# Two-layer convolution-attention kernel: which engine forms the neighbour sums of the second half of the batch, and in which order the second layer follows

## The reference, cut to what matters

```python
x = x + dilated_attention(group_norm(x))     # first layer
x = x + channel_attention(group_norm(x))     # second layer
```

```python
attn = softmax_over_9(q * shifted(k) summed over a head's channels * scale)
out  = sum_over_9(attn[n] * shifted(v, n)) * gate[s]
```

## Time and profile before

| what | value |
|---|---|
| device time, median of 3 runs | 83.1 us (83.1 to 83.11) |
| the profiled execution's own time | 83.13 us |
| span of that execution in the trace | 81.3 us |
| around the span (start and end) | 1.8 us |
| PE busy | 71.1 us (87%) |
| DVE busy | 67.5 us (83%) |
| POOL busy | 41.5 us (51%) |
| ACT busy | 29.3 us (36%) |
| share of the chain that ended last | DVE 54%, PE 28%, POOL 7% |

### The profile page before, as it was taken

The page is one execution under the profiler, slowest core; times in us unless marked ns, Lnnn a source line. Parts: engine busy times, 40 slices in busy tenths (PEclk is TensorE's granted clock), DMA queues, the critical chain, the costliest instruction groups (busy, mean ns, idle before and its releaser), DMA issues.

```text
span 81.3 us, 2474 instructions
## 1 busy us (share of the span) xinstructions
PE 71.1 (87%) x1010; PEld 51.4 (63%) x1010; DVE 67.5 (83%) x184; ACT 29.3 (36%) x92; POOL 41.5 (51%) x84
## 2 busy tenths in 40 slices
PE   4999998799995698999969797879999999999950
PEld 4999753466742466776857664567676868575530
DVE  2152999999999989999999699889999888597850
ACT  1762765963384000000030003230994271764200
POOL 7104018912930037999999999699990005100000
PEclk9999999999999999999999999999999999999999
DMA  1980055000000000000000000000000000012253
GB/s 27 315 286 18 0 120 142 7 0 8 0 0 4 0 12 0 0 0 4 8 0 0 0 0 0 8 0 0 0 0 8 0 0 12 0 57 72 73 194 129
DMA packets 2796, 3.06 MB, mean 38 GB/s; under 512 B 352, under 2 KB 2400, under 8 KB 2784
## 3 DMA queue, kind: packets, MB, share of 16 engines
q1 hardware_dynamic: 2496, 2.63, 10.5%
q10 hardware_dynamic: 288, 0.26, 0.9%
HBM read 1.84 MB, written 1.05 MB: 36 GB/s over the span
## 4 chain that ended last, share of the span: by engine, by line
DVE 54%; PE 28%; POOL 7%; issue 5%; ACT 2%; POOLq 0%
PE ps L815 27%; DVE qk L602 18%; DVE pv L643 12%; POOL rstd L342 3%; POOL acc L379 3%; DVE acc L655 3%; DVE pv L655 2%; DVE x L674 2%; DVE prob L622 2%; DVE smax L609 2%; DVE ssum L619 2%; POOL pv L379 2%; DVE sums L570 1%; DVE acc L643 1%; PE ps L972 1%
## 5 line engine op out<-in xcount | busy, mean ns | idle before, releaser
L815 PE MATMUL ps<-prob,sel 64*128 64x192 f32 (+6 forms) x192 | 17.8, 313 | 2.7 <-DVE pv L643 1.6
L643 DVE TENSOR_TENSOR pv<-ps,v 128x128 f32<-128x128 f32 (+7 forms) x32 | 17.1, 567 | 1.8 <-PE ps L815 0.8
L815 PEld LDWEIGHTS ps<-prob,sel 64*128 64x128 f32 x192 | 13.7, 186 | 6.9 <-DVE pv L643 3.5
L815 PE MATMUL ps<-xn,wp 128*32 128x256 f32 (+1 forms) x208 | 17.1, 384 | 0.9 <-ACT q L417 0.7
L815 PE MATMUL ps<-idle 128*128 128x128 f32 x82 | 14.6, 328 | 1.1 <-DVE idle L533 1.1
L379 POOL TENSOR_TENSOR pv<-pv 128x240 f32<-128x240 f32 (+3 forms) x24 | 14.1, 600 | 0.5 <-DVE pv L643 0.5
L815 PEld LDWEIGHTS ps<-idle 128*128 128x128 f32 x82 | 12.6, 231 | 2.4 <-DVE idle L533 1.1
L342 POOL TENSOR_TENSOR rstd<-gvar,mhalf 128x2 f32<-128x2 f32 (+1 forms) x6 | 4.9, 809 | 15.9 <-DVE gvar L549 15.9
L379 POOL TENSOR_TENSOR acc<-acc,pv 128x256 f32<-128x256 f32 (+4 forms) x20 | 12.7, 640 | 0.5
L815 PEld LDWEIGHTS ps<-xn,wp 128*32 128x32 f32 (+1 forms) x208 | 8.7, 116 | 6.1 <-ACT xn L443 1.3
L602 DVE TENSOR_TENSOR qk<-q,k 128x672 f32<-128x672 f32 (+7 forms) x21 | 11.4, 607 | 0.0
(11 more groups left out here) (82 smaller groups left out, 89.6 us busy)
## 6 DMA issues: line engine op xcount, KB each, us to landing
out_dram<-x SPq DMA_DIRECT2D x8, 128.0 KB, 1.8
gx<-x_dram SPq DMA_DIRECT2D x2, 256.0 KB, 4.4
gx<-x_dram ACTq DMA_DIRECT2D x2, 128.0 KB, 3.1
sel<-selc_dram SPq DMA_DIRECT2D x4, 64.0 KB, 2.2
wp<-wpack_dram SPq DMA_DIRECT2D x1, 194.0 KB, 4.2
gx<-x_dram SPq DMA_DIRECT2D x1, 192.0 KB, 2.8
wp<-wpack_dram SPq DMA_DIRECT2D x1, 131.0 KB, 2.2
gx<-x_dram SPq DMA_DIRECT2D x1, 128.0 KB, 3.0
```

What stands on the lines that cost most here:

```text
L643: last = nc.vector.tensor_tensor(o, a, b, ALU.mult)
L815: return nc.tensor.matmul(o, w, m, start=start, stop=stop)
```

## The change

PE takes over the sums of (1,2) and (1,3) almost wholly, and the second half of (0,3). POOL keeps all 8 additions of (0,0), (0,1), (0,2), (1,0), (1,1) and the first 4 of (0,3). DVE's 8 additions of (1,2) and 2 of (1,3) become 6 small ones behind its last product (`add_last`). `restore` and `sum_second` are replaced by `add_tiles`, which takes products in 32x32 tiles for phase 0 (all four slots j at once) and for phase 1 (two slots j at a time: first batches 1 and 3, then 5 and 7). PE's second-layer work of groups 0 and 1, but for two projections, moves behind these sums, and so does DVE's and ACT's; five calls of `keep_clock` on a group's bank go; one `norm` moves from ACT to DVE; the inverse roots of groups 0 and 1 stand behind other additions of POOL.

The bodies of the functions that go stand in the code above, and the indentation is shortened.

```diff
@@ -31,15 +31,15 @@
 X_PIECES = ((0,), (2,), (4,), (6,), (1, 3), (5, 7))
 ARRIVAL = (0, 2, 6, 4, 1, 3, 5, 7)
 X_ORDER = (0, 2, 4, 6, 1, 3, 5, 7)
-NORMS_ON_DVE = ((2, 0), (3, 0), (3, 1))
-NORMS_ON_ACT = ((0, 0), (0, 1), (1, 0), (1, 1), (2, 1))
+NORMS_ON_DVE = ((2, 0), (2, 1), (3, 0), (3, 1))
+NORMS_ON_ACT = ((0, 0), (0, 1), (1, 0), (1, 1))
 PT_ON_DVE = ((2, 0), (2, 1))
 PT_ON_ACT = ((0, 0), (0, 1), (1, 0), (1, 1), (3, 0), (3, 1))
 MT_ON_DVE = ((0, 0), (3, 1))
 MT_ON_ACT = ((0, 1), (1, 0), (1, 1), (2, 0), (2, 1), (3, 0))
-POOL_SUMS = (ND, 2)
-RSQRT_AFTER = ((1, 0, 4), (1, 1, 0))
+POOL_ADDS = ((8, 8, 8, 4), (8, 8, 0, 0))
+RSQRT_AFTER = ((1, 1, 1), (1, 1, 3))
 F32 = mybir.dt.float32
@@ -86,8 +86,12 @@
     return [(t, a, f) for (t, a), f in zip(pairs, after)]
-ADDS = len(additions(0))
 ADD_NEEDS = (1, 2, 2, 2, 3, 3, 3, 3)
+def added_by(ph, s):
+    return sum(POOL_ADDS[0]) * ph + sum(POOL_ADDS[ph][:s + 1])
 def valid_rows(s, ri):
@@ -217,7 +221,6 @@
 spread_ready = sem("spread_ready")
 pv_ready = sem("pv_ready")
 added = sem("added")
-dve_added = sem("dve_added")
 last_added = sem("last_added")
 restored = sem("restored")
 xn1_act_ready = sem("xn1_act_ready")
@@ -366,10 +369,10 @@
     link(nc.gpsimd.tensor_tensor(gsel[:], gpick[:, :, 0], gpick[:, :, 1], ALU.add))
     nc.gpsimd.tensor_tensor(gate[:], gsel[:], grec[:], ALU.mult).then_inc(gate_ready, 1)
-    base = 0
     for ph in range(PHASES):
-        for s in range(POOL_SUMS[ph]):
-            for n, (target, slot, after) in enumerate(additions(s)):
+        for s in range(ND):
+            base = added_by(ph, s) - POOL_ADDS[ph][s]
+            for n, (target, slot, after) in enumerate(additions(s)[:POOL_ADDS[ph][s]]):
                 chunk = 12 * ph + 3 * s + ADD_NEEDS[n]
                 if n == 0 or ADD_NEEDS[n] > ADD_NEEDS[n - 1]:
                     pool.wait_ge(pv_ready, chunk)
@@ -380,7 +383,6 @@
                 if (ph, s, n) in RSQRT_AFTER:
                     g = RSQRT_AFTER.index((ph, s, n))
                     rsqrt(PHASES + g, group(g))
-            base += ADDS
     for g in range(len(RSQRT_AFTER), GROUPS):
         rsqrt(PHASES + g, group(g))
@@ -492,29 +494,29 @@
     for i in range(2):
         norm(0, i)
     for i in range(2):
+        copy_projection(0, i)
+    for i in range(2):
         norm(1, i)
-    for i in range(2):
-        copy_projection(0, i)
-    copy_projection(1, 0)
-    for i in range(2):
-        copy_pT(0, i)
-    copy_projection(1, 1)
-    for i in range(2):
-        copy_pT(1, i)
-    attention_exp(0)
-    attention_exp(1)
     squares(2)
     squares(3)
+    for i in range(2):
+        copy_pT(0, i)
+    for i in range(2):
+        copy_projection(1, i)
+    copy_projection(2, 0)
+    attention_exp(0)
+    copy_projection(2, 1)
+    for i in range(2):
+        copy_pT(1, i)
+    for i in range(2):
+        copy_projection(3, i)
+    attention_exp(1)
     copy_fused(0, 1)
-    copy_fused(1, 0)
-    norm(2, 1)
-    copy_fused(1, 1)
-    for g in range(2, 4):
-        for i in range(2):
-            copy_projection(g, i)
-    copy_pT(3, 0)
+    for i in range(2):
+        copy_pT(3, i)
     attention_exp(2)
-    copy_pT(3, 1)
+    for i in range(2):
+        copy_fused(1, i)
     attention_exp(3)
     for i in range(2):
         copy_fused(2, i)
@@ -631,7 +633,9 @@
             dve.wait_ge(proj_copied, tiles.index((2, s, ph)) + 1)
         dve.wait_ge(spread_ready, c + 1)
         if ph and chunk == 0:
-            dve.wait_ge(added, ADDS * (s + 1))
+            dve.wait_ge(added, added_by(0, s))
+            if s == LAST_UNIT:
+                dve.wait_ge(restored, SLOTS)
         c0, c1, co = columns(DIL[s], ci)
         nc_ = c1 - c0
         for n, ri, dri, r0, dr, a0, da, rows in pieces(s):
@@ -643,27 +647,17 @@
             last = nc.vector.tensor_tensor(o, a, b, ALU.mult)
         last.then_inc(pv_ready, 1)
-    def add_neighbours(ph, s):
...
-    def add_last_column():
...
+    def add_last():
+        steps = ((2, 7, 6, 0), (3, 7, 6, 0), (2, 1, 0, 0), (2, 7, 8, 1), (3, 7, 8, 2), (2, 1, 2, 3))
         dve.wait_ge(pv_ready, 12 * PHASES)
-        for n, ri in enumerate((0, 2)):
+        for s, onto, slot, after in steps:
+            ci, ri = divmod(slot, 3)
             r0, r1 = valid_rows(s, ri)
-            c0, c1, _ = columns(DIL[s], 2)
-            o, a = (pv[s][:, slot, :].rearrange("p (r c) -> p r c", c=W)[:, r0:r1, c0:c1] for slot in (middle, 6 + ri))
-            if n:
-                dve.wait_ge(last_added, n)
+            c0, c1, _ = columns(DIL[s], ci)
+            o, a = (pv[s][:, n, :].rearrange("p (r c) -> p r c", c=W)[:, r0:r1, c0:c1] for n in (onto, slot))
+            if after:
+                dve.wait_ge(last_added, after)
             nc.vector.tensor_tensor(o, o, a, ALU.add).then_inc(last_added, 1)
     def first_residual(g):
@@ -764,40 +758,40 @@
         multiply_pv(1, 0, i)
     multiply_pv(1, 1, 0)
     first_residual(0)
-    multiply_pv(1, 1, 1)
+    first_residual(1)
+    for i in range(1, 3):
+        multiply_pv(1, 1, i)
     second_variance(0)
-    first_residual(1)
-    multiply_pv(1, 1, 2)
+    multiply_pv(1, 2, 0)
     second_variance(1)
-    for i in range(2):
-        multiply_pv(1, 2, i)
+    multiply_pv(1, 2, 1)
     second_norm_bias(0)
-    second_norm_bias(1)
     multiply_pv(1, 2, 2)
     multiply_pv(1, 3, 0)
-    add_neighbours(1, 2)
+    second_norm_bias(1)
     for i in range(1, 3):
         multiply_pv(1, 3, i)
-    add_last_column()
+    add_last()
+    first_residual(2)
+    second_variance(2)
+    first_residual(3)
+    second_norm_bias(2)
+    for i in range(2):
+        norm(2, i)
+    second_variance(3)
     attention_shift(0)
+    second_norm_bias(3)
+    for i in range(2):
+        norm(3, i)
+    attention_divide(0)
+    for i in range(2):
+        copy_pT(2, i)
+    copy_fused(0, 0)
     attention_shift(1)
-    attention_divide(0)
-    first_residual(2)
-    first_residual(3)
-    copy_fused(0, 0)
-    second_variance(2)
     attention_divide(1)
-    second_variance(3)
-    second_norm_bias(2)
-    norm(2, 0)
-    second_norm_bias(3)
-    for i in range(2):
-        norm(3, i)
-    copy_pT(2, 0)
-    second_residual(0, 0)
-    copy_pT(2, 1)
-    second_residual(0, 1)
     attention_shift(2)
+    for i in range(2):
+        second_residual(0, i)
     attention_divide(2)
     attention_shift(3)
     second_residual(1, 0)
@@ -913,43 +907,23 @@
             last = mm(o, sel[half:half + 64, j % 2, s, :], m)
         last.then_inc(spread_ready, 1)
-    def restore(g):
...
-    def sum_second():
...
+    def add_tiles(ph, tiles, js, stop, finished=False):
+        for s, slot in tiles:
+            if slot == 4:
+                t, first, (r0, r1), (c0, c1) = acc, (ph * ND + s) * N, (0, H), (0, W)
+            else:
+                ci, ri = divmod(slot, 3)
+                t, first, (r0, r1), (c0, c1) = pv[s], slot * N, valid_rows(s, ri), columns(DIL[s], ci)[:2]
             dims = [[W, r1 - r0], [1, c1 - c0]]
             at = r0 * W + c0
-            for j in range(SLOTS):
+            for j in js:
                 rows = slice(32 * j, 32 * j + 32)
-                last = mm(view(ps, 512 * (BANK[2] + j) + at, dims, 32 * s, 32), ident[rows, rows],
-                          view(t, first + at, dims, 32 * j, 32), start=start, stop=stop)
-                if stop and s == LAST_UNIT:
+                last = mm(view(ps, 512 * (BANK[GROUPS // PHASES * ph] + j) + at, dims, 32 * s, 32),
+                          ident[rows, rows], view(t, first + at, dims, 32 * j, 32),
+                          start=slot == 4, stop=(s, slot) in stop)
+                if finished and (s, slot) == tiles[-1]:
                     last.then_inc(restored, 1)
-        pe.wait_ge(pv_ready, 12 * PHASES)
-        pe.wait_ge(added, ADDS * sum(POOL_SUMS))
-        pe.wait_ge(dve_added, ADDS)
-        for s in range(ND):
-            tile(s, acc, (ND + s) * N, start=True, stop=s != LAST_UNIT)
-        s = LAST_UNIT
-        for slot in (3, 5, 1, 0, 2, 7):
-            ci, ri = divmod(slot, 3)
-            if slot == 7:
-                pe.wait_ge(last_added, 2)
-            tile(s, pv[s], slot * N, *valid_rows(s, ri), *columns(DIL[s], ci)[:2], stop=slot == 7)
     def group_stats(g):
         pe.wait_ge(sum_ready, B + GB * (g + 1))
@@ -1050,55 +1024,62 @@
     for i in range(3):
         spread(1, 0, i)
     spread(1, 1, 0)
-    restore(0)
+    pe.wait_ge(qk_ready, ND * PHASES)
+    pe.wait_ge(id_loaded, 16)
+    pe.wait_ge(pv_ready, 12)
+    pe.wait_ge(added, added_by(0, LAST_UNIT))
+    add_tiles(0, [(0, 4), (1, 4), (2, 4), (3, 4), (3, 1), (3, 7), (3, 6), (3, 8)], range(SLOTS),
+              stop=((0, 4), (1, 4), (2, 4), (3, 8)), finished=True)
     spread(1, 1, 1)
+    spread(1, 1, 2)
     group_stats(0)
-    restore(1)
-    spread(1, 1, 2)
+    spread(1, 2, 0)
     group_stats(1)
-    for i in range(2):
-        spread(1, 2, i)
-    keep_clock(2, BANK[1] + 1)
+    spread(1, 2, 1)
     spread(1, 2, 2)
```

(135 more changed lines are left out.)

12 lines of the change are left out of this document (6 added, 6 removed).

## The result

The changed kernel takes 89.43 us (median; 88.66 to 89.58) against 83.1 in the same session: ratio 1.076, 95% interval 1.068 to 1.083. I had forecast 84.1, with a range of 82.1 to 86.0. The profiled execution took 89.5 us with a span of 87.7. On its page PE's busy time is 5.2 us more than before, that of DVE, ACT and POOL is less, and the clock row shows why.

What follows compares the result with a forecast made beforehand. Neither PE nor DVE alone was the bound: DVE paced 49.56 to 63.69 us, PE the end from 70.85. Sections -2.2 + 1.7 - 1.15 + 2.6 gave about +1.0 us on 83.13, so 84.1, range 82.1 to 86.0.

Steps and rivals of the forecast that it cites:

- the clock falls: Rival: among the spreads of (1,2) PE's granted clock falls to 1.2 GHz, costing 2.4 us, 86.5 in all; chance 0.08.
- section A: From 49.56 us to DVE's last addition (before: 63.69): -2.2 us, mostly from DVE's neighbour additions going.
- Section B: From DVE's last addition to all of `x1` (before: 2.84 us): 4.5 us, so +1.7.
- Section C: From `x1` to group 3's first projection (before: 4.32 us): a chain of small steps takes 3.15 us, so -1.15.
- Section D: From group 3's first projection to the last residual (before: 8.21 us): PE gets 2.9 us of moved work, so +2.6.
- The first stall: Section A, ahead of DVE's last additions: DVE waits for a norm, projection and spread, +0.6 us.
- port waits: Section A: small DVE operations held while POOL adds, 0.9 us as before, so no difference; ends 0.9 less and 0.9 more.
- in single file: Section B: two pairs of slots go through PE one after the other, where before all four went at once.
- the second early pass: Section B: early products of the second pair of slots, 768 columns on PE, 1.3 us between residuals of groups 2 and 3.
- the moved work fits: Rival: PE's moved work falls mostly into gaps, section D adds 1.1 instead of 2.6, 82.6 us in all; chance 0.25.
- Tiles in strict order: Rival: a pass of two slots costs the sum over its products, not its longest tile; 3 us more, 87; chance 0.04.

Runs made afterwards that it cites:

- run 12: The kernel of run 11 without its three fillers (unused PE products) among the spreads of (1,2): 88.93 us.
- run 3: The kernel before the change without its three fillers among the spreads of (1,2): 82.93 us against 82.67, ratio 1.001.
- run 14: The kernel of run 11 with both projections of group 0 behind the last sums and transposes of groups 0 and 1 behind group 3's statistics: 85.32 us.
- run 1: The changed kernel with three fillers (unused products) put back among the spreads of (1,2): 83.89 us, ratio 1.013 to the kernel before.
- run 11: The kernel of run 9 with transposes, projections, variance and copies moved ahead in the queues of PE, DVE and ACT: 82.62 us, ratio 0.998 to the kernel before.
- run 8: The kernel of run 1 with the last products of all four slots at once, early products of both pairs ahead of them: 83.97 us.
- run 9: The kernel of run 8 with DVE taking the residuals of groups 2 and 3 ahead of the variance of group 2: 84.12 us.
- Run 7: The kernel of run 1 with each finish product of group 0 issued twice: 84.8 us against 83.89.
- run 2: The changed kernel with seven fillers (two and five) among the spreads of (1,2): 86.14 us.

## Why the prediction was wrong

*What failed is the weight and the price of the rival "the clock falls".* The sum itself has no term for the clock: each section is priced at its full level. I gave the rival 0.08 because the clock row of before showed no fall even around 24 to 28 us, where PE was busy 2.44 of 4 us. That row spoke of another stretch with other products, and it doesn't carry over: with 2.35 of 3.4 us in spreads and small statistics the clock fell in each of the four executions (mean clock 0.899 to 0.921), and again in run 12. The busy time of PE alone doesn't tell when it falls: in stretches of equal length the clock held with 2.29 us (run 3) and fell behind 2.54 (run 12) and 2.94 (run 14). I also looked at the fillers only as what kept the clock. Run 3 shows that the kernel before held it without them; the second `restore` may have done it, but no run tested that alone. So what the new order lacked in 51 to 56 us stays open, but for this: three fillers there are enough to keep the clock in that stretch (runs 1 and 11 against the changed kernel and run 12). The price, 2.4 us, took the fall to last for eight products in section A. It lasted 17 us: 2.4 us more in A, 2.1 in B, 1.2 in C (windows of the changed kernel less those of run 1), 5.7 together.

*The sum itself held.* By the windows of run 1:
- Section A: -2.2 forecast, 11.69 against 14.13 measured, -2.4. That it is this near is in part luck, since three errors offset each other. The first residual started at 49.56, at the same time as in the kernel before, and not 0.35 later. The first stall (0.6 forecast) was no stall of its own. And four port waits of DVE cost some 1.65 us in place of 0.9.
- Section B: +1.7 forecast, 4.44 against 2.84, +1.6. The size is right, the reading "in single file" only in part: the two passes overlap (1.58 us in place of 1.95). That changes nothing, because the wait for the squares of group 2, which I had at 2.5 us behind the last addition, does end there (63.73 less 61.25), now with 0.85 us of idle time, and the last products of the second pair are queued behind it. Undone (runs 8 and 9), the order gives 1.4 us at `x1`, which reaches the end only when the queues behind are changed too (run 11).
- Section C: -1.15 forecast, 3.16 against 4.32, -1.15.
- Section D: +2.6 forecast, 11.06 against 8.21, +2.85. Run 7 shows that PE is the bound there, so the rival "the moved work fits" falls. DVE got 1.8 us more there (8.31 against 6.51 us busy), not some 3.
- Together +0.85 by the windows (79.91 against 79.06), +0.8 by the profiled executions (83.9 against 83.13), 1.2 by the medians on run 1's chip.

*Tiles in strict order.* By its own prices (1.3 us for the last products of one pair, 2.8 for the second early pass) run 1 would show 4.1 us from 61.30; it shows 1.58. This rival falls. The rival had joined two things, the rule of the Trainium skill ("TensorE: Matmul & The Clock Gate", Part 3, "The mechanism") that matmuls start and end in strict program order, and that a product's halves are issued together. So at least one of the two doesn't hold here, and the rows of run 1 speak against the rule itself. In the program the products of (2,7), 192 columns, stand ahead of those of (1,4), 256 columns of `acc`. For the second pair, from 64.05 us on (a row can merge two widths):

```profile
64.05 0.40 PE L809 MATMUL ps<-acc,cs 32*32 32x256 f32 x2
64.16 0.37 PE L809 MATMUL ps<-pv,cs 32*32 32x128 f32 x4
64.29 0.38 PE L809 MATMUL ps<-acc,cs 32*32 32x256 f32 x2
64.36 0.49 PE L809 MATMUL ps<-pv,cs 32*32 32x192 f32 x4
```

All four MATMULs of (1,4) have started by 64.3, and the last four of 192 columns, those of (2,7), only then. That holds as far as the program's order is the order of issue, which the trace doesn't show.

*Port waits.* In run 1 the variance and bias operations of groups 0 and 1 took 0.54 to 0.60 us in four of six cases, and 0.14 to 0.16 in the other two. The four:

```profile
52.86 0.56 DVE L551 SCALAR_TENSOR_TENSOR gvar<-gst,gsq 128x2 f32<-128x2 f32 x1
54.32 0.60 DVE L550 TENSOR_TENSOR gsq<-gst 128x2 f32<-128x2 f32 x1
54.95 0.59 DVE L551 SCALAR_TENSOR_TENSOR gvar<-gst,gsq 128x2 f32<-128x2 f32 x1
57.72 0.54 DVE L557 TENSOR_TENSOR nbias<-gst,rstd 128x2 f32<-128x2 f32 x1
```

The whole-instruction lock that the Trainium skill ("SBUF — State Buffer", section "SBUF: two separate sides") describes agrees with those. Their cost over 0.16 us each is 1.65 us, 0.75 more than I took, which lay inside my bounds. My remark that the small operation ahead of the one at 54.40 was not held is no evidence against a lock: in the kernel before it started at 54.21, and POOL's addition only at 54.22.

## What to carry to other kernels

When an edit takes work from PE, ask of each thin stretch that it leaves what held the granted clock there; a page without a fall doesn't say how near one was. A few unused products (here three, which made PE busy 3.02 in place of 1.89 us in 52.40 to 55.80) can be worth 5 us, and a fall can last far beyond the thin stretch ahead of it. And an earlier result is worth nothing while the next engine's queue has a waiting instruction at its head: move the gain through each queue behind it, or it is given back.

## What the runs showed of the hardware

The clock, once low, stayed low for 17 us with PE busy 15.85 of 16.00, mostly in 32x32 products of identity columns, spreads and projections; in run 2 it was back after 3.4 us. What ends a fall is open, and so is which property of PE's work brings one on: no run varied only that, and the busy time ahead of a fall (1.89 of 3.42 us in the changed kernel, 2.94 of 3.4 in run 14) doesn't set it apart from stretches in which the clock held (2.29 of 3.4 in run 3). Products of different 32x32 tiles ran side by side across two passes: 384 and 768 columns in their longest tiles, over in 1.58 us, where the two one behind the other are 1.95 at the prediction's 1.7 ns a column. By the rows of 64.05 to 64.36 they also didn't start in the order of the program.
